# Order of words, counts, sorting and collecting in a graph-pooling kernel

## What is computed

```
mask = A != 0;  rank = cumsum(mask) - 1;  num_nbr = mask.sum(axis=1)
m_i = where(num_nbr > 5, ceil(num_nbr / 2), 1)
keep = mask & ~((rank + 1) % m_i == 0)
svals = sort(where(keep[:, :, None], x[None], big), axis=1)
agg = mean over q in (0.25, 0.5, 0.75) of svals[ceil(q * n_keep) - 1]
out = (0.5 * agg + 0.5 * x) @ W.T + b + x
```

## Time and profile before

| | us |
|---|---|
| median of 3 timed runs | 164.19 (163.62 to 164.71) |
| the profiled execution | 162.21 |
| its span | 160.4 |
| busy: PE / DVE / ACT / POOL | 99.6 / 103.3 / 110.6 / 71.8 |
| mean granted clock of TensorE | 0.83 of full |

### The profile page before, as it was taken

One profiled execution on the slowest core, in us unless ns is written; L12 is line 12 of the kernel. 1 busy time (PEld: TensorE's weight loads), 2 busy tenths in 40 slices (PEclk: granted clock), 3 DMA queues, 4 the chain that ended last, 5 costly groups with the idle time before them and its releaser, 6 DMA issues.

```text
span 160.4 us, 2105 instructions
## 1 busy us (share of the span) xinstructions
PE 99.6 (62%) x552; PEld 51.5 (32%) x553; DVE 103.3 (64%) x450; ACT 110.6 (69%) x137; POOL 71.8 (45%) x118
## 2 busy tenths in 40 slices
PE   0001964893985980594369239647667898865962
PEld 0000332341232340242124114223225786644441
DVE  1002287226855269899741989959999979999900
ACT  3088888888898777887878888766799444441021
POOL 6897000000077770577820047774773078560030
PEclk9999999558558598589956965997589999999697
DMA  5999999999999999999999999999940143312002
GB/s 154 420 425 430 428 431 428 431 428 419 420 428 411 398 399 401 425 420 395 410 405 418 425 425 411 411 411 385 392 146 6 49 115 100 90 34 68 0 6 67
DMA packets 9571, 49.99 MB, mean 312 GB/s; under 512 B 1715, under 2 KB 5307, under 8 KB 6230
## 3 DMA queue, kind: packets, MB, share of 16 engines
q1 hardware_dynamic: 7648, 47.71, 73.3%
q0 software_dynamic: 1760, 2.07, 4.3%
q10 hardware_dynamic: 150, 0.07, 0.2%
HBM read 49.61 MB, written 1.71 MB: 320 GB/s over the span
## 4 chain that ended last, share of the span: by engine, by line
DMA 52%; DVE 19%; PE 10%; issue 7%; POOL 5%; ACT 3%; SPq 1%; POOLq 0%; DVEq 0%
DMA adj<-in_adj 48%; POOL gath_b L458 4%; DMA gath_b<-in_table,idx_b 4%; PE ps_w L816 3%; PE ps_w L658 3%; ACT sq L513 2%; DVE rec L902 1%; DVE quads_b L1008 1%; DVE quads_b L1010 1%; DVE merged L1010 1%; DVE merged L1008 1%; DVE hot L891 1%; PE ps_out L714 1%; DVE quads_a L1010 1%; POOL gath_a L458 1%
## 5 line engine op out<-in xcount | busy, mean ns | idle before, releaser
L513 ACT ACTIVATE sq<-adj 128x3328 bf16<-128x3328 int32 x26 | 77.4, 2977 | 21.9 <-DMA adj<-in_adj 21.9
L658 PE MATMUL ps_w<-sq,hot 128*128 128x416 bf16 x208 | 59.0, 442 | 4.4 <-DVE hot L891 4.2
L458 POOL DMA_INDIRECT gath_a<-in_table,idx_a x12 | 12.4, 1030 | 49.7 <-DVEq L967 47.0
L658 PEld LDWEIGHTS ps_w<-sq,hot 128*128 128x128 bf16 x208 | 20.7, 118 | 28.2 <-issue 16.8
L458 POOL DMA_INDIRECT gath_b<-in_table,idx_b x24 | 25.1, 1045 | 7.3 <-issue 7.3
L891 DVE SCALAR_TENSOR_TENSOR hot<-slot_code,ps_place,strip_unit 128x256 bf16<-128x256 f32 (+1 forms) x22 | 11.0, 535 | 21.2 <-PE ps_place L636 20.4
L458 POOL DMA_INDIRECT gath_s<-in_table,idx_s x16 | 17.4, 1087 | 12.1 <-DVE idx_s L955 7.8
L891 DVE SCALAR_TENSOR_TENSOR hot<-slot_code,ps_out,strip_unit 128x256 bf16<-128x256 f32 (+1 forms) x22 | 11.0, 535 | 14.7 <-PE ps_out L636 13.7
L629 PE MATMUL ps_place<-level,mpart 64*128 64x2 bf16 x13 | 2.3, 175 | 23.9 <-ACT classes L523 23.9
L629 PE MATMUL ps_out<-level,mpart 64*128 64x2 bf16 x13 | 2.3, 178 | 23.2 <-ACT classes L523 23.2
L629 PEld LDWEIGHTS ps_place<-level,mpart 64*128 64x128 bf16 x13 | 1.2, 96 | 29.7 <-ACT classes L523 17.2
(11 more groups left out here) (275 smaller groups left out, 191.4 us busy)
## 6 DMA issues: line engine op xcount, KB each, us to landing
adj<-in_adj SPq DMA_DIRECT2D x26, 1664.0 KB, 12.6
out<-res SPq DMA_DIRECT2D x6, 192.0 KB, 2.1
xT<-in_xT SPq DMA_DIRECT2D x1, 896.0 KB, 17.8
xT<-in_xT SPq DMA_DIRECT2D x1, 768.0 KB, 15.6
gath_b<-in_table,idx_b POOLq DMA_INDIRECT x24, 6.2
gath_s<-in_table,idx_s POOLq DMA_INDIRECT x16, 2.8
out<-res SPq DMA_DIRECT2D x1, 256.0 KB, 2.3
out<-res SPq DMA_DIRECT2D x2, 128.0 KB, 1.9
```

Of the source, the lines that this page charges most:

```text
L458: nc.gpsimd.indirect_dma_start(slots[:, k, :], None, x_table, bass.IndirectOffsetOnAxis(ap=indices[:, k:k + 1], axis=0), bounds_check=TABL ...
L513: nc.scalar.activation(sq_ring[t % RING][:], adj_ring[t % RING][:], ACT.Square, accum_out=meta[:, t, 0:1]).then_inc(s_sq, 1)
L658: last = nc.tensor.matmul(ps_w[b % 2][h][:, 0:HW], hot[t % 3][:, s, :], sq_ring[t % RING][:, first:first + HW], start=False, stop=end and ...
```

## The change

Six things move; no operation is added or removed.

1. TensorE: words(t) now stand ahead of the count of t+1 for all tiles but 7, 12, 14, 18 and 19 (`COUNT_FIRST`).
2. VectorE: the first sorting layers of the second pair, `sort_b(1)`, go from tile 19 to tile 17, ahead of the lists of block 5 and of the third pair; its merge goes from tile 20 to 19, its pooling from 21 to 20.
3. VectorE: `pool_a(2)` goes from tile 23 to tile 21, ahead of `list_words(6)`.
4. VectorE: `pool_b` is cut in two; for the third pair the ends come at tile 24, ahead of hot(25), the picks stay behind it.
5. TensorE: `collect_mid` goes from behind `own_part(2)` to ahead of `turn(2)`.
6. VectorE: the first minimum of the first lone block's sort comes ahead of the wait for `mrec` instead of behind it.

```diff
-WORDS_FIRST = (5, 11, 17)
+COUNT_FIRST = (7, 12, 14, 18, 19)
...
             for t in range(NT):
-                if t + 1 < NT and t not in WORDS_FIRST:
+                if t + 1 < NT and t in COUNT_FIRST:
                     count_places(t + 1)
                 if t == BLOCKS[block_of(t)][0]:
                     number_words(block_of(t))
                 fill_words(t)
-                if t in WORDS_FIRST:
+                if t + 1 < NT and t not in COUNT_FIRST:
                     count_places(t + 1)
...
             listed_part(1)
+            collect_mid()
             turn(2)
             own_part(2)
-            collect_mid()
             listed_part(2)
...
-            def pool_b(j):
+            def pool_b_ends():
 
                 S, T = merged, order
                 v.tensor_tensor(T[:, 3, :], S[:, 3, :], S[:, 4, :], ALU.max)
                 step(v.tensor_tensor(T[:, 0:3, :], S[:, 3:8:2, :], S[:, 4:9:2, :], ALU.min))
+
+            def pool_b_picks(j):
+                T = order
...
                 if t == 17:
+                    sort_b(1)
                     list_words(5)
                     list_pair(2)
...
                 if t == 14:
-                    pool_b(0)
+                    pool_b_ends()
+                    pool_b_picks(0)
                 if t == 15:
                     list_words(4)
                 if t == 19:
-                    sort_b(1)
+                    merge()
                 if t == 20:
-                    merge()
+                    pool_b_ends()
+                    pool_b_picks(1)
                 if t == 21:
-                    pool_b(1)
+                    pool_a(2)
                     list_words(6)
                 if t == 22:
                     list_alone(0)
                 if t == 23:
-                    pool_a(2)
                     sort_b(2)
                 if t == 24:
                     merge()
+                    pool_b_ends()
...
-            pool_b(2)
+            pool_b_picks(2)
...
-            dve.wait_ge(s_mrec, 1)
-            copied = did(v.tensor_copy(mrec[:], ps_mrec))
             dve.wait_ge(s_gath_s[0], KEYS * 16)
             did(v.tensor_tensor(pb[:, :, 0, :], pg[:, :, 0, :], pg[:, :, 1, :], ALU.min))
-            need(copied)
+            dve.wait_ge(s_mrec, 1)
+            step(v.tensor_copy(mrec[:], ps_mrec))
```

## The result

Paired with the kernel before on one chip, the changed kernel took 167.87 us in the median (166.96 to 168.75, 4 runs) against 163.91 (162.34 to 164.71, 4 runs): ratio 1.0253, 95% interval 1.0158 to 1.0349. The change makes the kernel slower by 2.5%. The forecast had the sign (165.3 us, 163.2 to 167.0) and less than half of the size. The profiled execution took 168.75 us, span 167.0, against 162.21 and 160.4 before. In this document a median is over all executions of a kernel, while a ratio compares only those within 1.5% of its fastest, so that some ratios are not the quotient of the two medians.

What follows compares the result with a forecast made beforehand. The start of the third pair's lists was taken to set the end, through 12 serial gathers on POOL. Terms +1.0 - 0.1 + 0.25 + 0.1 = +1.25 us, taken as 1.1 on the median 164.19: 165.3 us, range 163.2 to 167.0.

Steps and rivals of the forecast that it cites:

- `collect_mid` earlier, quads ahead of `mrec`: Tail after `list_words(7)`: VectorE gains about 1.0 us but loses it waiting for TensorE, delayed 1.05, mostly absorbed; net +0.1 us.
- Rival 1: TensorE at 1.2 GHz for words(25): +1.36 us, in all 166.7; 168 with the second list up to 2 late; chance 0.27.
- Rivals 2 and 3: 2: slow words(17) in timed runs, no change, 164.0 us, chance 0.18; 3: second pair lands before 84.75, 162.5 us, chance 0.12.
- Rival 4: Words are held by hot matrices, not counts: TensorE's new order changes nothing, the +1.0 us stays; no chance of its own.

Runs made afterwards that it cites:

- u_sort: Changed kernel with the second pair's sort, merge and pooling back at tiles 19, 20 and 21; 165.77 us, ratio 1.0171 to the kernel before.
- u_collect: Changed kernel with items 5 and 6 undone (`collect_mid` and the first minimum back in their old places); 164.18 us, ratio 1.0102 to the kernel before.
- b_56: Kernel before with items 5 and 6 only; 164.5 us, ratio 1.0103; run again 164.91 us, 1.0102.
- b_5: Kernel before with only `collect_mid` moved ahead of `turn(2)`; 164.93 us, ratio 1.0102.
- p_fetch: Kernel before with items 5 and 6 and 20 always satisfied waits in VectorE's queue; 168.07 us where the kernel before took 168.93, no ratio of its own.
- n_16: Kernel before with only words(16) moved ahead of the count of tile 17; 163.92 us, ratio 0.9971.
- w_gap: Kernel before with items 5 and 6, SyncE's write of block 5 held until the last lone block's gathers landed; 168.07 us, 0.9974; again 165.26 us, 1.0154.
- u_ends: Changed kernel with the third pair's ends back behind hot(25); 172.88 us, ratio 1.027, where the kernel before took 168.93.
- w_tail: Changed kernel with 8 of the 16 warming matmuls ahead of the wait for `slow_n` and 8 behind; 171.45 us, ratio 1.0151 to the kernel before.
- u_order: Changed kernel with TensorE's old order of words and counts; 168.61 us, ratio 1.0381 to the kernel before.
- k_clock: Changed kernel with ten constant matmuls, result unread, ahead of words(24) and words(25); 167.64 us, ratio 1.0211 to the kernel before.
- b_6: Kernel before with only the first minimum moved ahead of the copy of `mrec`; 162.99 us, ratio 0.9959.
- warm_8: Kernel before with the first minimum ahead of `mrec` and 8 of 16 warming matmuls ahead of the wait for `slow_n`; 160.96 us, ratio 0.9841.
- f_order: Kernel before with only TensorE's new order of words and counts; 162.96 us, ratio 1.0002.
- f_sort: Kernel before with only the second pair's sort moved to tile 17, its merge to 19 and pooling to 20; 164.65 us, ratio 1.0052.

## Why the prediction came out too low

**What held.** The walk along the waits was right to a tenth up to the third pair's last issue, and again in `turn(2)`:

| step | forecast | profile after |
|---|---|---|
| landing of pair two, VectorE's wait | 86.68, 1.9 | 86.72, 1.91 |
| `list_words(5)` | 89.2 | 89.26 |
| last gather of pair three issued | 109.55 | 109.61 |
| its landing | 115.4 | 115.98 |
| landing to `list_words(7)` | 9.2, or 10.56 at the low clock | 10.64; 9.27 and 9.26 in `u_sort` and `u_collect` |
| `list_words(7)` to `turn(2)` | 5.5 | 5.46 |
| `list_words(7)` to `slow_n` | 23.5 (23.42 before, and 0.1) | 25.37 |

The third pair's landing came 0.6 late: the last gather took 6.37 us, not the 5.85 interpolated between two single rows, of a kind that scatters from 5.9 to 7.0 in the earlier trace rows. Without the step that failed, `u_collect`, the change costs 1.0102, which is 1.7 us of 163.91 (0.6 to 2.7); the forecast for the same steps was 1.15.

**The step that failed** is "`collect_mid` earlier, quads ahead of `mrec`", put at +0.1 net of a gain of 1.0 on VectorE and a loss of 1.05 on TensorE. Three runs put it at 1.0% alone, some 1.7 us (`b_56` twice, `b_5`), and its removal from the whole takes the ratio from 1.0253 to 1.0102. Both halves of the reasoning failed. TensorE's loss was never felt: in the profile after it waits 1.61 us for VectorE at `slow_sum`. VectorE's gain of 1.0 was there (0.95), but there was a bound that I had not read: the last lone block's gather. The prediction's rows of the tail hold TensorE and VectorE and not POOL. POOL's eight issues start from `list_alone(1)`, which the step does not touch, and the last ends in a landing at 140.4, where VectorE arrived at 140.41. So with POOL's issues as they were the gain was zero from the outset, and any lateness of that gather would count in full. It was late: 0.36 us by POOL's issues and 1.04 by the completion in `b_56`; 0.36 and 1.59 in the changed kernel (141.56 to 145.47, 3.91 us), which is the +1.95 of the table above. That second part I could not have had from the profile of before. A zero gain, and a range to above, I could.

Why the completion is later stays open. It goes with `collect_mid`'s place: it was 2.9 to 3.9 us from issue to use in twelve of the thirteen profiles with the new place (all with a wait) and 2.5 in `p_fetch`; with the old place it was 2.6 in the one that had a wait (`n_16`, 0.21), and in the six others VectorE took the data without a wait after 2.3 or 2.4. Holding back the gathers behind it or the write beside it did not take the loss away. Nor does the loss come everywhere: in the rounds where the kernel before took 168.93 us, VectorE did not get ahead, POOL's issues were not longer, and `w_gap`, which has both moves, cost nothing (0.9974).

**Rival 1, the low clock for the last words,** came in the profiled execution, with its 1.36 us and by the place that it named, and it is not a fixed part of the change: `u_collect`, which differs from the changed kernel only behind words(25), ran six of them in 1.22 us, as did `u_sort`, `u_ends` and `w_tail`; `u_order`, `k_clock` and, with none of the early steps of the change, `p_fetch` took 2.24. Its second half, a late second list, is what `u_order` showed (`list_words(5)` at 90.38) and `k_clock` (90.45). In kernels with the old place of the sort the second list came as late as 61.70 to 62.31 in three profiles (`b_6`, `warm_8`, `b_5`) and the third list was still at 88.06, 86.44 and 86.40. The old order on VectorE absorbs that lateness; with the change it passes on whole (0.99 late at the second list and 1.12 at the third in `u_order` against the changed kernel). I had put the second list's shift at 0, from one profile in which it was early. This may be why the whole costs more (2.5%) than its two measured parts added (1.0% and 1.0%), but no run separates that, and the interval of the whole (1.6 to 3.5%) takes in 2.0%.

**Rivals 2 and 3** did not come: the kernel got slower, and the second pair landed at 86.72, not before 84.75. **Rival 4**, that the new order on TensorE changes nothing, held: `f_order`, 1.0002.

**The Trainium skill**, "DMA: Bandwidth & Descriptors", in the section on the anatomy of a DMA on the gpsimd path, would give a gather that fills its 64 KB 2.15 us, an estimate. 64 KB is the room for 128 rows; the gathers' queue moved 2.07 MB in all 55 transfers, 38 KB each on average, which changes the estimate by less than 0.1. Once the stream is over and with `collect_mid` in its old place the trace is near it (2.3 us for the last gather, up to 3.5 for the eight of the last lone block); beside the stream the traces show 5.9 to 7.0, as in the earlier trace rows, and after `collect_mid`'s move up to 3.9 for the last one. The landing that the rule has at 82.7 came at 86.72. The Trainium skill, "TensorE: Matmul & The Clock Gate", Part 1, says that the clock's changes fall differently from run to run. The traces agree: one kernel, `b_56`, 13.30 and 15.27 us from `slow_n` to the end.

**The base.** The prediction took the profiled execution as a lucky one and was right to; it then moved the sum on the median unchanged. The profile after is an unlucky one (168.75, the slowest of its four): two single profiles would give 4.0%, the paired runs give 2.5%.

## What to carry to other kernels

Before work is moved ahead on an engine, read at every point where the engine takes data from a DMA how long before that the data landed, marked wait or not: a landing that is only just hidden turns the gain into a wait. Work put ahead of a list into "free" waiting time ties that list to its own input; whatever makes this input late from run to run, and the old order absorbed, now reaches the end. And look at warming matmuls as at any other work: the eight that ran in a wait of TensorE cost nothing here, the 16 behind it stood on the path.

## What the runs showed of the hardware

- The last gather of the tail took 2.3 to 2.6 us from issue to use with `collect_mid` in its old place, and 2.9 to 3.9 in twelve of thirteen profiles with that one group of 16 small matmuls moved ahead on TensorE. The cause is unknown. Its packets hold about 0.01 MB; beside the stream, gathers of up to 64 KB took 5.9 to 7.0 us to land.
- POOL's issue of a gather takes 1.00 us and 0.30 between two, but single ones take longer. Of the last lone block's eight, the third and fourth took 1.43 each in the kernel before, `f_sort` and `u_collect`; the third took 2.24 and the fourth 1.00 in `b_56`, `u_order` and the changed kernel. It does not hang on `collect_mid`'s place alone: `b_6` has 1.00 and 1.43, and `p_fetch`, `w_gap` at first and `w_tail`, with the new place, have 1.39 to 1.46 for both.
- Ten matmuls of 416 columns (six ahead of words(24), four ahead of words(25)) did not bring the clock back (six words 2.24 us as before).
- The clock in the last 13 to 15 us alone is worth 2 us: 16 warming matmuls took 4.45 or 5.72 us, the last eight 1.13 or 1.96, in one and the same kernel.
